# Float32 projections of two attention stages turned into three float32r passes, with the low halves subtracted on VectorE and GpSimd

## What is computed

```python
def _self_attention(x, wq, bq, wk, bk, wv, bv, wo, bo):
    q = ((x @ wq + bq) * HEAD_DIM ** (-0.5)).reshape(b, s, N_HEADS, HEAD_DIM)
    k = (x @ wk + bk).reshape(b, s, N_HEADS, HEAD_DIM)
    v = (x @ wv + bv).reshape(b, s, N_HEADS, HEAD_DIM)
    p = jax.nn.softmax(jnp.einsum('bqhd,bkhd->bhqk', q, k), axis=-1)
    return jnp.einsum('bhqk,bkhd->bqhd', p, v).reshape(b, s, d) @ wo + bo
```

## Time and profile before

| | |
|---|---|
| median of 3 runs | 5286.25 us (5284.78 to 5296.24) |
| profiled execution | 5298.91 us, span of its instructions 5297.2 us |
| TensorE matmul busy | 4926.9 us (93%), 45659 instructions |
| TensorE weight loads | 4001.1 us (76%) |
| VectorE busy | 3899.7 us (74%) |
| ScalarE busy | 3865.1 us (73%) |
| GpSimd busy | 2027.2 us (38%) |
| mean granted TensorE clock | 0.98 of full speed |

### The profile page before, as it was taken

One profiled execution on the slowest core, in us unless ns is written; L12 is line 12 of the kernel. 1 busy time (PEld: TensorE's weight loads), 2 busy tenths in 40 slices (PEclk: granted clock), 3 DMA queues, 4 the chain that ended last, 5 costly groups with the idle time before them and its releaser, 6 DMA issues. The chain is left out here.

```text
span 5297.2 us, 147856 instructions
## 1 busy us (share of the span) xinstructions
PE 4926.9 (93%) x45659; PEld 4001.1 (76%) x45660; DVE 3899.7 (74%) x9253; ACT 3865.1 (73%) x8215; POOL 2027.2 (38%) x1692
## 2 busy tenths in 40 slices
PE   0999999979999999889999999995799999999998
PEld 0777777758888888667777777773599999899997
DVE  7888888868888888689999999997744444344433
ACT  5899999958888888767777777773655555555554
POOL 1222232313333333234444444442144544444443
PEclk9999999989999999999999999997799999999999
DMA  6777777746666666467777777772432332323222
GB/s 189 184 188 187 190 186 189 187 125 194 196 196 197 196 197 197 138 170 185 186 185 186 183 185 186 185 185 70 52 64 47 63 57 45 64 49 64 47 47 28
DMA packets 631700, 750.63 MB, mean 142 GB/s; under 512 B 143365, under 2 KB 560334, under 8 KB 631472
## 3 DMA queue, kind: packets, MB, share of 16 engines
q1 hardware_dynamic: 575136, 679.62, 49.0%
q0 software_dynamic: 49152, 63.09, 7.3%
q10 hardware_dynamic: 7184, 5.00, 0.3%
HBM read 476.49 MB, written 272.24 MB: 141 GB/s over the span
## 5 line engine op out<-in xcount | busy, mean ns | idle before, releaser
L1762 POOL DMA_INDIRECT out_dram<-exp_gated,exp_token x256 | 419.7, 1639 | 717.6 <-ACT exp_gated L1666 377.1
L1011 DVE TENSOR_REDUCE F_tops<-F_score 128x2 f32<-128x512 f32 x1024 | 668.8, 686 | 22.6 <-PE F_score L706 14.3
L1712 DVE TENSOR_TENSOR exp_hT_lo<-exp_whole,exp_hT_hi 128x512 fp32r<-128x512 f32 x512 | 355.4, 694 | 437.1 <-ACT exp_hT_hi L1655 437.1
L871 ACT ACTIVATE F_probs<-F_scoreT 128x512 f32<-128x512 f32 x1024 | 571.4, 591 | 74.7 <-PE F_scoreT L677 73.4
L1011 DVE TENSOR_REDUCE A_tops<-A_score 128x3 f32<-128x384 f32 x1024 | 526.9, 553 | 83.9 <-PE A_score L696 65.5
L1615 PE MATMUL exp_res<-exp_w_hi,exp_hT_hi 128*128 128x256 f32 x2048 | 573.5, 280 | 0.0
L1617 PE MATMUL exp_res<-exp_w_lo,exp_hT_hi 128*128 128x256 f32 x2048 | 568.0, 277 | 0.0
L1618 PE MATMUL exp_res<-exp_w_hi,exp_hT_lo 128*128 128x256 f32 x2048 | 567.9, 277 | 0.0
L1666 ACT ACTIVATE exp_gated<-exp_y,exp_gate 128x256 f32<-128x256 f32 x256 | 109.4, 498 | 624.1 <-DVE exp_y L1736 594.5
L871 ACT ACTIVATE A_probs<-A_scoreT 128x384 f32<-128x384 f32 x1024 | 463.3, 481 | 17.2 <-PE A_scoreT L665 8.8
L1602 PE MATMUL exp_hid<-exp_xT_hi,exp_w_lo 128*128 128x512 f32 x1024 | 405.9, 396 | 0.0
(11 more groups left out here) (355 smaller groups left out, 14326.1 us busy)
## 6 DMA issues: line engine op xcount, KB each, us to landing
QS<-d_q SPq DMA_DIRECT2D x384, 192.0 KB, 3.7
KS<-d_k SPq DMA_DIRECT2D x256, 192.0 KB, 4.0
QS<-d_q SPq DMA_DIRECT2D x384, 128.0 KB, 3.8
KS<-d_k SPq DMA_DIRECT2D x256, 128.0 KB, 4.0
d_q<-A_q_parts SPq DMA_DIRECT2D x64, 384.0 KB, 3.0
d_k<-A_k_parts SPq DMA_DIRECT2D x64, 384.0 KB, 2.8
QS<-d_q SPq DMA_DIRECT2D x384, 64.0 KB, 3.6
d_q<-X_q_parts SPq DMA_DIRECT2D x64, 384.0 KB, 2.6
```

Source lines behind the costliest of these rows:

```text
L871: nc.scalar.activation(probs[m][0:KR, at:at + HB, :].rearrange("p u x -> p (u x)"), scoreT[i % TB][0:KR, 0:HB * TCOL], ACT.Exp)\
L1011: nc.vector.tensor_reduce(dst, src, AX.X, ALU.max).then_inc(score_read, 1)
L1712: v.tensor_tensor(hT_lo[:, f, :], whole[f % OB][:, :], hT_hi[:, f, :], ALU.subtract).then_inc(h_split, 1)
L1762: nc.gpsimd.indirect_dma_start(out, bass.IndirectOffsetOnAxis(token[j % (2 * XB)][:, s:s + 1], 0), gated[par][:, s, :], None, bounds_check ...
```

## The change

- In stages 2 and 3 the operands of q and proj, and in stage 3 of k and v, are split into a high half, rounded to float32r by a ScalarE copy, and a low half, the difference. `product` issues three float32r matmuls (high by high, high by low, low by high) in place of one float32 matmul.
- The weights are split once per stage, ahead of its loop. In stage 3 the gain of the layer norm is multiplied into wq, wk and wv by GpSimd, and its bias goes through them into new biases `bias_qk` and `bias_v`, by matmuls and VectorE.
- Stage 2: ScalarE's copies of xT0, xT1 and aT no longer release the PSUM bank; VectorE subtracts the high half from PSUM (xT_lo, aT_lo) and releases it. VectorE's string gets xT0, aT and xT1.
- Stage 3: ScalarE copies xT and aT from PSUM twice, once rounded to float32r and once in float32 (xT_f, aT_f), and GpSimd subtracts. GpSimd's string gets xT and aT between refetch and q. TensorE waits for these in q and proj.
- The buffers QS, KS and others move from the whole program into the stages. Rows 96 and 97 of KS are filled by two DMAs per stage instead of by GpSimd once. Constants are allocated in another order, and those of the early stages are given back ahead of stage 3.

The diff, cut to what matters:

```diff
-        for kb in C["KS"]:
-            nc.gpsimd.memset(kb[96:98, :], -1.0).then_inc(pooled, 1)
-        pool.wait_ge(pooled, 15)
+        nc.gpsimd.memset(C["minus"][:, :], -1.0).then_inc(pooled, 1)
+        pool.wait_ge(pooled, 14)
...
-"DVE": ("topB v mcopy maxima tok0 tok1 norm maxima maxima maxima maxima topA wo stats maxima var c0 c1 "
+"DVE": ("topB v mcopy maxima tok0 tok1 norm maxima xT0 maxima aT xT1 maxima maxima topA wo stats maxima var c0 c1 "
...
-"POOL": ("k_rest refetch q q_rest uapply k"),
+"POOL": ("k_rest refetch xT aT q q_rest uapply k"),
...
-    QS, V = C["QS"], C["V"]
-    KS = [t[:, 0:H * KP].rearrange("p (h x) -> p h x", h=H) for t in C["KS"]]
+    V = C["V"]
...
-xdt = BF16 if kind == "A" else F32
-xin, grid = sb("xin", [P, 2, 256]), sb("grid", [P, 2, 256])
-xw, xT = sb("xw", [P, 2, 256], xdt), [sb(f"xT{i}", [P, 2, 256], xdt) for i in range(2)]
...
+QS, KS = [sb(f"QS{i}", [98, H, 256], BF16) for i in range(2)], [sb(f"KS{i}", [98, H, KP], BF16) for i in range(2)]
+xin = sb("xin", [P, 2, 256])
+xw = sb("xw", [P, 2, 256], BF16 if kind == "A" else F32)
+xT = [sb(f"xT{i}", [P, 2, 256], BF16 if kind == "A" else F32R) for i in range(2)]
...
+if kind != "A":
+    xT_lo = [sb(f"xT_lo{i}", [P, 2, 256], F32R) for i in range(2)]
+    aT, aT_lo = sb("aT", [P, 2, 256], F32R), sb("aT_lo", [P, 2, 256], F32R)
+    xres, based, summed = sb("xres", [P, 2, 256]), sb("based", [P, 2, 256]), sb("summed", [P, 2, 256])
+    w_hi = [sb(f"w_hi{i}", [P, 2, 256], F32R) for i in range(4 if kind == "F" else 2)]
+    w_lo = [sb(f"w_lo{i}", [P, 2, 256], F32R) for i in range(4 if kind == "F" else 2)]
+    w_scaled, w_high, w_split, x_cast, a_cast = (sem(n) for n in ("w_scaled", "w_high", "w_split", "x_cast", "a_cast"))
...
+padded, filled = sem("padded"), sem("filled")
...
+    zres, xT_f, aT_f = sb("zres", [P, 2, 256]), sb("xT_f", [P, 2, 256]), sb("aT_f", [P, 2, 256])
+    x_split, a_split = sem("x_split"), sem("a_split")
+    bias_qk, bias_v, b_wide = sb("bias_qk", [P, 2, 2]), sb("bias_v", [P, 512]), sb("b_wide", [P, 2, P])
+    widened, shifts, bias_ready = sem("widened"), sem("shifts"), sem("bias_ready")
...
+        def fill():
+            for t in KS:
+                sp.dma_start(t[96:98, :, :], C["minus"][:, 0:KP].unsqueeze(1).broadcast_to([2, H, KP])).then_inc(filled, 16)
...
         for b, par in iterations(sp):
+            if isinstance(b, int) and b == FIRST + 1:
+                fill()
...
     def _(pe):
         mm = nc.tensor.matmul
-        wq, wk, wv, wo = C["w" + kind]
...
+            wq, wk, wv = (C["wT"][:, i, :, :] for i in range(3))
+        if kind == "X":
+            wk, wv = C["xk"], C["xv"]
+            (wq, wo), (wq_lo, wo_lo) = w_hi, w_lo
         if kind == "F":
+            (wq, wk, wv, wo), (wq_lo, wk_lo, wv_lo, wo_lo) = w_hi, w_lo
+            pe.wait_ge(widened, 2)
+            for i in range(2):
+                for m in range(2):
+                    for c in range(2):
+                        mm(work[0][:, 2 * i + m:2 * i + m + 1], C["wF"][i][:, c, m * P:(m + 1) * P], C["ln1_b"][:, c:c + 1],
+                           start=i + m + c == 0, stop=c == 1, skip_group_check=True)
+            for c in range(2):
+                last = mm(work[0][:, 256:512], b_wide[:, c, :], C["wF"][2][:, c, :], start=False, stop=c == 1,
+                          skip_group_check=True)
+            last.then_inc(shifts, 1)
+            pe.wait_ge(bias_ready, 4)
             pe.wait_ge(wr_ready, 1)
+
+        def product(out, rows, columns, start, stop):
+
+            (a, a_lo), (b, b_lo) = rows, columns
+            mm(out, a, b, start=start, stop=False)
+            mm(out, a, b_lo, start=False, stop=False)
+            return mm(out, a_lo, b, start=False, stop=stop)
+
         if kind == "X":
             for s in score:
...
                     if kind != "X":
                         drained("xT")
+                        if kind == "F":
+                            pe.wait_ge(x_split, g + 1)
...
+                    if kind != "A" and isinstance(g, int) and g == 0:
+                        pe.wait_ge(w_split, len(w_lo))
                     for m in range(2):
                         for c in range(2):
-                            last = mm(W[:, m * 256:m * 256 + n], w[:, c, m * P:(m + 1) * P], src[:, c, 0:n],
-                                      start=c == 0, stop=c == 1)
+                            ms = slice(m * P, (m + 1) * P)
+                            if kind == "A" or (kind == "X" and name == "k"):
+                                last = mm(W[:, m * 256:m * 256 + n], w[:, c, ms], src[:, c, 0:n],
+                                          start=c == 0, stop=c == 1)
+                            else:
+                                w_rest = wq_lo if name == "q" else wk_lo
+                                last = product(W[:, m * 256:m * 256 + n], (w[:, c, ms], w_rest[:, c, ms]),
+                                               (src[:, c, :], xT_lo[gp][:, c, :]), c == 0, c == 1)
...
                     else:
                         for j in range(2):
                             for c in range(2):
-                                last = mm(W[:, j * 256:(j + 1) * 256], xT[gp][:, c, j * P:(j + 1) * P], wv[:, c, :],
-                                          start=c == 0, stop=c == 1)
+                                js = slice(j * P, (j + 1) * P)
+                                if kind == "A":
+                                    last = mm(W[:, j * 256:(j + 1) * 256], xT[gp][:, c, js], wv[:, c, :],
+                                              start=c == 0, stop=c == 1)
+                                else:
+                                    last = product(W[:, j * 256:(j + 1) * 256],
+                                                   (xT[gp][:, c, js], xT_lo[gp][:, c, js]),
+                                                   (wv[:, c, :], wv_lo[:, c, :]), c == 0, c == 1)
...
                 elif name == "proj":
                     drained("aT")
+                    if kind == "F":
+                        pe.wait_ge(a_split, g + 1)
                     for j in range(2):
                         for c in range(2):
-                            last = mm(W[:, j * 256:(j + 1) * 256], aT[:, c, j * P:(j + 1) * P], wo[:, c, :],
-                                      start=c == 0, stop=c == 1)
+                            js = slice(j * P, (j + 1) * P)
+                            last = product(W[:, j * 256:(j + 1) * 256], (aT[:, c, js], aT_lo[:, c, js]),
+                                           (wo[:, c, :], wo_lo[:, c, :]), c == 0, c == 1)
...
+        if kind == "X":
+            for i, w in enumerate((C["xq"], C["xo"])):
+                nc.scalar.activation(w_hi[i][:, :, :], w[:, :, :], ACT.Copy).then_inc(w_high, 1)
+        if kind == "F":
+            act.wait_ge(w_scaled, 6)
+            for i, w in enumerate(C["wF"]):
+                nc.scalar.activation(w_hi[i][:, :, :], w[:, :, :], ACT.Copy).then_inc(w_high, 1)
...
                 elif name in ("xT0", "xT1"):
-                    last = nc.scalar.activation(xT[gp][:, int(name[2]), :], W[:, 0:256], ACT.Copy)
+                    nc.scalar.activation(xT[gp][:, int(name[2]), :], W[:, 0:256], ACT.Copy).then_inc(x_cast, 1)
+                    continue
                 elif name == "xT":
                     drained(g - 2, "v")
-                    for c in range(2):
-                        last = nc.scalar.activation(xT[gp][:, c, :], W[:, c * 256:(c + 1) * 256], ACT.Identity,
-                                                    bias=C["ln1_b"][:, c:c + 1], scale=C["ln1_g"][:, c:c + 1])
+                    turned = W[:, :].rearrange("p (c t) -> p c t", c=2)
+                    need(act, x_split, g)
+                    nc.scalar.activation(xT[gp][:, :, :], turned, ACT.Copy).then_inc(x_cast, 1)
+                    last = nc.scalar.activation(xT_f[:, :, :], turned, ACT.Copy)
...
+                    if kind == "F" and isinstance(g, int) and g == 0:
+                        act.wait_ge(bias_ready, 4)
...
-                            bias = C["bq_f" if name == "q" else "bk_f"][:, m:m + 1]
+                            bias = bias_qk[:, "qk".index(name), m:m + 1]
...
                 elif name == "aT":
                     drained(g - 1, "proj")
-                    last = nc.scalar.activation(aT[:, :, :], W[:, :].rearrange("p (c t) -> p c t", c=2), ACT.Copy)
+                    turned = W[:, :].rearrange("p (c t) -> p c t", c=2)
+                    nc.scalar.activation(aT[:, :, :], turned, ACT.Copy).then_inc(a_cast, 1)
+                    if kind == "X":
+                        continue
+                    need(act, a_split, g)
+                    last = nc.scalar.activation(aT_f[:, :, :], turned, ACT.Copy)
                 elif name == "h2T":
...
+        if kind == "F":
+            for c in range(2):
+                nc.vector.tensor_copy(b_wide[:, c, :], C["ln1_b"][:, c:c + 1].broadcast_to([P, P])).then_inc(widened, 1)
```

(37 more changed lines are left out.)

58 lines of the change are left out of this document (30 added, 28 removed).

## The result

The changed kernel takes 5718.48 us (median of 4 runs, 5709.93 to 5729.32) against 5287.09 us before (4 runs beside it): 1.0814 times the time, 95% interval 1.0791 to 1.0836. It is slower, as forecast, but by 431 us and not 226: the forecast of 5512 us (5400 to 5590) is missed.

What follows compares the result with a forecast made beforehand. Both stages were taken as close to bound by two engines at once, each in a strict order. Terms 134 + 90 + 2 = 226 us gave 5525 us profiled, 5512 us as median; range 5400 to 5590.

Steps and rivals of the forecast that it cites:

- The step that failed: Stages 2 and 3: TensorE's granted clock stays at 1.00, so q behind the waits takes 1.36 us.
- The second step that failed: Stage 3: GpSimd's two added subtractions hold VectorE for 0 us, at most 1.16 us each in the range.
- the walk: Stage 3, one batch traced: q starts 2.4 us later, next scores come 2.05 us late, VectorE is 1.05 us late.
- Projection: Stages 2 and 3: 12 float32r matmuls take 1.36 us instead of 1.73, a gain of 0.37 us per projection.
- Stage 2's handover: VectorE's subtractions release banks late, next score 2.4 us later; 2.1 us a batch taken, 134 us in all.
- Stage 3's handover: TensorE's q waits 2.4 us for GpSimd's xT subtraction; 1.4 us a batch taken, 90 us in all.
- GpSimd holds VectorE: Rival, stage 3: both new subtractions hold VectorE every batch, 148 us on top, 5660 us; chance 0.06.
- Once per stage: Work outside the loops, mainly scalings, subtractions and copies before stage 3: 2 us taken, 0 to 14 for the range.
- TensorE as the bound: Rival, stages 2 and 3: TensorE bounds, handovers come early enough, gains of 47 and 70 us, 5169 us; chance 0.07.
- Only stage 2 pays: Rival: stage 3's wait shrinks to 1.2 us, less than the 1.48 gained; 5410 us; chance 0.15.

Runs made afterwards that it cites:

- filler: Changed kernel plus useless bf16 matmuls in TensorE's two long waits (ahead of aT and yT in stage 2, q in stage 3), handovers as late: 5577.92 us.
- unwaited3: Changed kernel, but stage 3's products take high halves for the turned rows' low halves, without waiting for subtractions; all added work stays: 5541.03 us, stage 3 1330.1 us.
- high_only: Changed kernel with high halves in place of the turned rows' low halves, three passes kept; their subtractions, second casts and waits left out: 5237.69 us.
- order23b: Changed kernel, nothing left out, with VectorE's strings in stages 2 and 3 and GpSimd's and TensorE's in stage 3 reordered: 5401.80 us.
- order23c: Against order23b: in stage 2 ScalarE takes a seed before yT and TensorE a maxima before q; in stage 3 TensorE a maxima before h2T: 5418.21 us.
- two_pass: Against high_only: two float32r passes per product instead of three, rows rounded once, weights in both halves, no subtractions or waits for rows' low halves: 5235.68 us.

## Why the forecast was wrong

**The step that failed** is "The trace shows the clock granted at 1.00 in both stretches, so I leave it there." The clock of a stretch belongs to the stalls of that stretch, and the change adds stalls. I had worked out that TensorE would stand idle for about 2 us in each batch, and went on to price q at full speed behind it. The filler run prices this step at 70.1 us in stage 2 and 74.9 in stage 3, 145 us together. The filler run's 5577.92 us are inside the forecast range, so this step alone made the miss.

**The second step that failed** is in stage 3, and the number hides it: "The new ones run while VectorE waits for the scores anyway, so 0 is taken". With the clock back at full (filler) stage 3 is 106.4 us longer than before, against 90 forecast. But the walk had VectorE 1.05 us late for scores in each batch, and there VectorE waits for scores for 2.3 us in 35 batches. What grew is its busy time, by 102.0 us, by being held. The cost that I walked isn't in that trace, and the cost that I put at 0 is there in its place, about as large: that the term fits is luck. The held time and the handover are not independent, as the wait decides which instructions GpSimd's meet: with the hold but no wait (unwaited3) stage 3 takes only 5.9 us more than in the kernel before.

**The sizes,** without those 145 us, lie near the slow ends of their bounds, one just outside:

| term, us | forecast | bounds | measured without the clock |
|---|---|---|---|
| stage 2 | 134 (2.1 a batch) | 1.4 to 2.5 | 224.7 - 70.1 = 154.6 (2.4) |
| stage 3 | 90 (1.4 a batch) | 0.95 to 1.7 | 181.3 - 74.9 = 106.4 (1.7) |
| around the stages | 2 | 0 to 14 | 14.8 |
| sum | 226 | | 275.8, and 145 for the clock |

- *Projection.* 1.73 us became 1.52 for proj and 1.49 to 1.52 for the others at full clock, not 1.36: the starts are about 0.126 us apart on average (the first gap 0.19, the others 0.12), where the last stage's passes had 0.113. The gain is 0.21 to 0.24 us, not 0.37, and this term was mis-sized by its row. Stage 2's q took 1.80 us before, not 1.73 (1706.51 - 1704.71), and gains 0.27. In high_only, with all passes and no handover, the time falls by 61 us.
- *Stage 2's handover.* The places and the mechanism were right: aT waits 1.89 us (2.06 walked), and without the clock the stage is 154.6 us longer, 2.4 a batch. VectorE's side of it in filler: it is busy for (944.7 - 856.8) / 64 = 1.4 us a batch more, with the three subtractions, and in 1500:2100 (32 batches) it waits 0.85 us for ScalarE's copy of aT, which the walk had between two of its steps, and waits 1.45 us for scores where it waited 1.1. The 2.91 us of the changed kernel's batch include the half clock of q.
- *Stage 3's handover.* q waits 2.40 us, as walked. VectorE's waiting for scores was forecast as 1.05 us a batch; the 1.2 us of the changed kernel look like it, but they are there only with q at half clock, and are 0.1 in filler.
- *GpSimd holds VectorE.* The hold hits topA, which stands ahead of the wait for scores, so the cover I named was not over it. It is worth 0.79 us a batch against high_only where nothing waits (unwaited3), and 102.0 / 64 = 1.6 us of VectorE's time against the kernel before in filler. The rival had 2.3 us on top of the handover's 1.4; what is there stands in place of the 1.4. A term of 0 was too small, 148 us on top too large.
- *Once per stage.* 13.6 us ahead of the two stages, not 2; high_only, which has the weights' halves and biases but no handovers, has 2.2 and 6.7 of it, 8.9 us together.
- *Rivals.* TensorE as the bound (5169 us) needs the handovers to be free, and even then, in high_only, the time is 5237.69: VectorE stops it in stage 3. "Only stage 2 pays" fails, as stage 3's wait stayed at 2.40 us and did not shrink to 1.2.

**What stays open.** What bounds the two stages in order23b (1085.0 and 1354.1 us, against 1009.1 and 1279.5 without handovers) is not settled. In stage 3 VectorE has 167 us of rest, so it is no longer the bound. In stage 2 the 0.7 us wait of `yT` for `aT_lo` is one candidate, and order23c's moves near it made things worse. No order that was tried keeps all halves and beats the kernel before: the best is 5401.80 us.

## What to carry to other kernels

When a change makes TensorE wait in every round of a loop, price the wait and then the work behind it at half clock until a trace shows otherwise; here this was a third of the whole loss, and work of no use put into the wait bought it back. Where an engine's order is strict, ask of a new handover which instruction it stands behind, before asking what it costs: moving a few names in three strings gave back 260 of 431 us. And a reading that an engine "is busy for all 200 us" doesn't make it the bound: take work off it alone, as two_pass does, and see whether the time follows. Last, a sum that comes out near the measured one doesn't show its terms: look in the trace for the wait that each term stands for.
